# Graph network on one core: search for node ends inside the first attention stage, longer lags and a batch ring in the edge stages, bank halves in a normalisation

## What is computed

```python
# layer 0, attention, summed by src over 4 heads
scores = clip(einsum('ehd,ehd->eh', q[src], k[dst]), -10, 10)
w = exp(scores) / segment_sum(exp(scores), src)[src]
x = layernorm(2 * x + segment_sum(w * v[dst], src))
# layer 1, sum: relu(x[src] + attr @ We + be) summed by dst, two matmuls, batch norm, relu
# layer 2, max: twice leaky_relu(segment_max(x[src] @ Wm + attr @ We, dst) + x @ Wr + b)
# layer 3, attention by dst: e = exp(leaky(a_src[src] + a_dst[dst]) - segment max)
out = tanh(segment_sum(h[src] * e, dst) / segment_sum(e, dst) + bias)
```

## Time and profile before

| | |
|---|---|
| time, median of 3 runs | 11399.82 us (11399.76 to 11401.9) |
| the profiled execution: run, span | 11406.15 us, 11404.3 us |
| busy share PE / PEld / DVE / ACT / POOL | 39% / 26% / 58% / 12% / 71% |
| granted TensorE clock, mean | 0.56 of full speed |
| DMA, mean over the span | 111 GB/s |
| e0, 578 to 2698 us | DMA engines 78% busy, 203 GB/s |

### The profile page before, as it was taken

One profiled execution on the slowest core, in us unless ns is written; L12 is line 12 of the kernel. 1 busy time (PEld: TensorE's weight loads), 2 busy tenths in 40 slices (PEclk: granted clock), 3 DMA queues, 4 the chain that ended last, 5 costly groups with the idle time before them and its releaser, 6 DMA issues. The chain is left out here.

```text
span 11404.3 us, 81326 instructions
## 1 busy us (share of the span) xinstructions
PE 4465.4 (39%) x15877; PEld 3003.7 (26%) x15877; DVE 6589.5 (58%) x11020; ACT 1415.8 (12%) x3304; POOL 8115.1 (71%) x8559
## 2 busy tenths in 40 slices
PE   3167666663222222243232323332323234444443
PEld 3066656662111111121111111111111123333332
DVE  9966666666555555555555555555555555555555
ACT  3011111111000000010000000000000023333333
POOL 2177777776777777757777776777777777777776
PEclk8555555555555555565555555555555555555665
DMA  3177788774333333323333333333333323333332
GB/s 96 57 200 206 205 203 205 205 204 124 98 99 98 99 99 98 91 71 98 100 98 99 98 100 80 98 99 99 98 99 98 95 60 81 82 82 81 81 83 68
DMA packets 1061469, 1264.91 MB, mean 111 GB/s; under 512 B 489075, under 2 KB 841315, under 8 KB 1060611
## 3 DMA queue, kind: packets, MB, share of 16 engines
q0 software_dynamic: 303968, 521.40, 20.5%
q1 hardware_dynamic: 638571, 636.33, 17.4%
q10 hardware_dynamic: 118432, 101.99, 3.6%
HBM read 830.35 MB, written 428.44 MB: 110 GB/s over the span
## 5 line engine op out<-in xcount | busy, mean ns | idle before, releaser
L825 POOL DMA_INDIRECT e_got<-kv_tab,dst_cols x1664 | 1584.1, 952 | 518.1 <-issue 507.3
L1106 POOL DMA_INDIRECT e2a_got<-x_tab,src_cols x1616 | 1524.8, 944 | 566.6 <-issue 566.6
L1763 POOL DMA_INDIRECT e_got<-h_tab,src_tcols x1616 | 1532.4, 948 | 502.5 <-issue 502.5
L1106 POOL DMA_INDIRECT e2b_got<-x_tab,src_cols x1616 | 1524.8, 944 | 512.0 <-issue 512.0
L1106 POOL DMA_INDIRECT e_got<-x_tab,src_cols x1616 | 1524.7, 944 | 507.3 <-issue 507.3
L835 PE MATMUL e_Q<-e_window,e_pick 128*128 128x96 f32 x3328 | 797.3, 418 | 696.9 <-issue 442.5
L1122 PE MATMUL e_EA<-we_We,e_attr 128*128 128x384 f32 x808 | 577.4, 870 | 1072.3 <-DVE e_emsg L1141 1072.3
L1122 PE MATMUL e2a_EA<-we_W_edge,e2a_attr 128*128 128x384 f32 x808 | 579.9, 873 | 1056.5 <-DVE e2a_emsg L1141 1056.5
L1122 PE MATMUL e2b_EA<-we_W_edge,e2b_attr 128*128 128x384 f32 x808 | 581.0, 874 | 1051.7 <-DVE e2b_emsg L1141 1051.7
L835 PEld LDWEIGHTS e_Q<-e_window,e_pick 128*128 128x128 f32 x3328 | 713.9, 317 | 803.2 <-issue 600.2
L1141 DVE TENSOR_TENSOR e2b_emsg<-e2b_EA,e2b_got 128x768 f32<-128x768 f32 x202 | 192.9, 955 | 728.4 <-issue 711.5
(11 more groups left out here) (368 smaller groups left out, 10371.3 us busy)
## 6 DMA issues: line engine op xcount, KB each, us to landing
scan_out<-e_out SPq DMA_DIRECT2D x416, 200.0 KB
e_window<-q_tab SPq DMA_DIRECT2D x1664, 48.0 KB
scan_out<-e_out SPq DMA_DIRECT2D x404, 196.0 KB
scan_out<-e_out SPq DMA_DIRECT2D x202, 384.0 KB
scan_out<-e2a_out SPq DMA_DIRECT2D x202, 384.0 KB
scan_out<-e2b_out SPq DMA_DIRECT2D x202, 384.0 KB
e_rel<-rel_row ACTq DMA_DIRECT2D x416, 128.0 KB
e_keep<-keep_row ACTq DMA_DIRECT2D x416, 100.0 KB
```

Of the source, the lines that this page charges most:

```text
L825: e.indirect_dma_start(got[u][:, k, :], None, kv_tab, bass.IndirectOffsetOnAxis(dst_c[:, c * K + k:c * K + k + 1], axis=0)).then_inc(s_g[u ...
L1106: e.indirect_dma_start(got[s % RS][:, k, :], None, x_tab, bass.IndirectOffsetOnAxis(src_cols[:, q:q + 1], axis=0)).then_inc(edge_got[s % R ...
L1763: e.indirect_dma_start(got[c % RG][:, k, :], None, h_tab, bass.IndirectOffsetOnAxis(src_tcols[:, q:q + 1], axis=0)).then_inc(s_g[c % RG], 16)
```

## The change

- find0 disappears as a stage; its work runs inside e0. The first src of each chunk is taken from first_row. ScalarE instead of VectorE counts, with Sign and an accumulator: one row count per chunk at chunks 8 to 56, one count in a gathered row at every second chunk from 84. GpSimd issues a search gather after the chunk's four at every second chunk from 80. VectorE makes the masks at chunk 6 and the ends at chunk 186. The masks' loads are issued by SP behind the windows of chunk 3, their stores behind those of chunk 39.
- In e0 the gather ring has six chunks, pick, rel and pay four buffers, the scan runs three chunks behind, queries three ahead, one-hot four ahead, SP's stores 13 behind the windows; a mask row holds two chunks.
- n3b hands over by halves (tiles 0 to 3, 4 to 6): matmuls, statistics, table and X.
- e3: gathers go straight into a ring of three batches (12 chunks), `hold` and its copies are gone; 1612 instead of 1616 gathers. Batch it is worked out in four pieces between the four chunks of batch it-1. The scan runs two chunks behind, the copies out further, and weights go to SBUF through ACT.
- In prep one GpSimd operation on 49 columns is dropped (node_q keeps its half).

```diff
-        with Phase("find0", group="node") as ph:
...
-        with Phase("e0", group="edge") as ph:
+        with Phase("e0", group="edge") as ph, Phase("find0", group="node") as pf:
+            QL, SL, RG0 = 3, 3, RG
...
+            ROWS_AT, GOT_AT, KEEP_AT = 8, 80, 6
+            COUNT_AT = GOT_AT + 4
+            END_AT = COUNT_AT + 2 * NT + 4
...
                 @block.sync
+                    BEHIND = 13
                     for c in range(NCH0):
...
-                        if c >= U:
-                            store(c - U)
+                        if c >= BEHIND:
+                            store(c - BEHIND)
+                        if c == U - 1:
+                            e.dma_start(dst_i[:, :], t["dst_pad"].rearrange("(p c) -> p c", p=P)).then_inc(s_dst, 16)
+                            e.dma_start(prev_i[:, :], t["dst_prev"].rearrange("(p c) -> p c", p=P)).then_inc(s_dst, 16)
...
                 @block.gpsimd
                     for c in range(NCH0):
-                        after(e, v_pay, c - U + 1)
+                        after(e, v_pay, c - RG0 + 1)
...
+                        if GOT_AT <= c < GOT_AT + 2 * NT and (c - GOT_AT) % 2 == 0:
+                            q = (c - GOT_AT) // 2
+                            e.wait_ge(a_row, q // G + 1)
+                            after(e, a_cnt, q - G + 1)
+                            e.indirect_dma_start(found[:, q % G, :], None, src_lin.rearrange("(r c) -> r c", c=CH),
+                                                 bass.IndirectOffsetOnAxis(row_i[:, q:q + 1], axis=0)).then_inc(row_got[q % G], 16)
...
                 @block.tensor
                     for c in range(NCH0):
...
-                        if c > 0:
-                            turn_back(c - 1)
-                        if c + 2 < NCH0:
-                            queries(c + 2)
+                        if c + QL < NCH0:
+                            queries(c + QL)
+                        if c >= SL:
+                            turn_back(c - SL)
...
                 @block.vector
-                        if c + 2 < NCH0:
-                            picks(c + 2)
-                        if c > 0:
-                            scan(c - 1)
+                        if c + 4 < NCH0:
+                            picks(c + 4)
+                        if c >= SL:
+                            scan(c - SL)
+                        if c == KEEP_AT:
+                            masks()
+                        if c == END_AT:
+                            ends()
...
                 @block.scalar
+                        if ROWS_AT <= c < ROWS_AT + NT:
+                            rows_of(c - ROWS_AT)
+                        if COUNT_AT <= c < COUNT_AT + 2 * NT and (c - COUNT_AT) % 2 == 0:
+                            count((c - COUNT_AT) // 2)
...
             with Phase("n3b", group="prep") as p2:
...
+                HALVES = ((0, 4), (4, G))
...
-                            after(e, a_x, it - 1)
-                            after(e, v_tab, it - 1)
-                            for g in range(G):
-                                q = it * G + g
-                                ins = e.matmul(raw(it, g), xT_all[:, q * P:(q + 1) * P], Wyi[:, :], start=True, stop=True)
-                            ins.then_inc(t_out, 1)
+                            for h, (lo, hi) in enumerate(HALVES):
+                                after(e, a_x, 2 * it + h - 3)
+                                for g in range(lo, hi):
+                                    q = it * G + g
+                                    ins = e.matmul(raw(it, g), xT_all[:, q * P:(q + 1) * P], Wyi[:, :], start=True, stop=True)
+                                ins.then_inc(t_out, 1)
...
         with Phase("e3", group="edge") as ph:
...
                 @block.gpsimd
+                    for q in range(TILES):
+                        it, c = q // BT, q // K
+                        if q % K == 0:
+                            after(e, v_add, c - RB * U + 1)
+                        e.indirect_dma_start(got[:, q % (RB * BT), :], None, h_tab, bass.IndirectOffsetOnAxis(src_tcols[:, q:q + 1], axis=0)).then_inc(s_g[it % RB], 16)
...
                 @block.vector
...
+                    batch = (logits, carries, maxima, factors)
+                    for it in range(NI + 1):
                         for u in range(U):
+                            c = (it - 1) * U + u
+                            if it > 0:
+                                add(c)
+                                if c > 1:
+                                    scan(c - 2)
+                            if it < NI:
+                                batch[u](it)
```

More of the change, by code:

```diff
@@ L1792, in batch, with spread @@
-                    def batch(it):
-                        H.wait(e, f"hold{U - 1}", it)
-                        TB.give(e.transpose(ST, hold[:, :, D + 1], ident[:, :]), "scores")
+                    def spread(c):
+                        it, u = c // U, c % U
+                        if u == 0:
+                            VB.wait(e, "low", it)
+                        after(e, v_scan, c - 2)
+                        for k in range(K):
+                            e.matmul(Z[c % 3][0:HW, k * P:(k + 1) * P], sel[:, u * K + k, :], parts[it % 2][:, :], start=True, stop=True)
@@ L1902, in body, with factors @@
[L1902 to L1910 removed]
+                    def factors(it):
+                        p = parts[it % 2]
+                        e.wait_ge(a_exp, it + 1)
+                        op(e.tensor_copy(p[0:BT, :], wd[:, 1, :]), it, "high")
+                        op(e.tensor_tensor(z[:, :], wd[:, 1, :], p[0:BT, :], ALU.subtract), it, "rest")
+                        op(e.tensor_copy(mid[:, :], z[:, :]), it, "mid")
+                        VB.give(e.tensor_copy(p[32:32 + BT, :], mid[:, :]), "mid32")
+                        VB.give(e.tensor_tensor(p[64:64 + BT, :], z[:, :], mid[:, :], ALU.subtract), "low")
@@ L1928, in body @@
-                    def body(it):
-                        for u in range(U):
-                            if not isinstance(it, int) or it > 0:
-                                step(it, u)
-                            c = it * U + u
-                            e.wait_ge(s_g[c % RG], got_before[c % RG] + 16 * K * (c // RG + 1))
-                            V[u].wait(e, "add", it, 1)
-                            H.give(e.activation(hold[:, u * K:(u + 1) * K, :], got[c % RG][:, :, :], ACT.Copy), f"hold{u}")
-                        VB.wait(e, "d", it)
-                        H.give(e.activation(wd[:, :, :], wd[:, :, :], ACT.Exp), "exp")
@@ L1938, in _, with to_out, message @@
-                    loop(e, NI, body, apart=4)
-                    for u in range(U):
-                        step(NI, u)
-                    to_out(NI + 1, 0)
+                    def to_out(c):
+                        e.wait_ge(t_back, c + 1)
+                        if c >= U:
+                            e.wait_ge(s_st[c % U], 16 * (c // U))
+                        e.activation(out[c % U][:, :, :], B[c % 2][:, 0:K * HW].rearrange("p (k d) -> p k d", k=K), ACT.Copy).then_inc(a_out, 1)
+                    def message(c):
+                        e.wait_ge(t_fwd, c + 1)
+                        after(e, v_scan, c - 2)
+                        e.activation(msg[c % 3][:, :], M[c % 2][0:HW, :], ACT.Copy).then_inc(a_msg, 1)
@@ new lines, in _ @@
+                    for it in range(NI + 1):
+                        for u in range(U):
+                            c = (it - 1) * U + u
+                            if c > 0:
+                                message(c - 1)
+                            if c > 3:
+                                to_out(c - 4)
+                            if u == 2 and it < NI:
+                                VB.wait(e, "d", it)
+                                e.activation(wd[:, :, :], wd[:, :, :], ACT.Exp).then_inc(a_exp, 1)
+                        if it < NI:
+                            TB.wait(e, "weights", it)
+                            e.activation(wts[it % 2][:, :], WT, ACT.Copy).then_inc(a_wt, 1)
@@ L1944, in build @@
+                    message(NCH - 1)
+                    for c in range(NCH - 4, NCH):
+                        to_out(c)
         with Phase("n7", group="node") as ph:
```

584 lines of the change are left out of this document (279 added, 305 removed).

## The result

The changed kernel takes 11480.5 us (median of 4 runs, 11479.1 to 11483.2) beside 11400.1 us for the kernel before on the same chip: ratio 1.007, 95% interval 1.0058 to 1.0082. A second set on another chip gave 11467.5 against 11398.8, ratio 1.0062 (1.0046 to 1.0079). The prediction of 11356 was wrong in its sign. The profiled execution spans 11479.1 us, against 11404.3.

What follows compares the result with a forecast made beforehand. GpSimd's issue of gathers was taken to bound the edge stages. Search and e0 -37.6, n3b -6 and e3 -0.3 summed to -43.9 us, giving 11356 us; range 11338 to 11380.

Steps and rivals of the forecast that it cites:

- the ring gives nothing inside: In e3, a ring of batches saves nothing between gathers; only four padding gathers left out, -5.0 us.
- Rival 3: In e0, VectorE's comparison L865 locks onto GpSimd's gather beat, 0.25 us per hit: 11445 us, slower; chance 0.03.
- Search in e0: Removing find0 puts e0's first gather at about 488.6, 89.7 us earlier; 49 search gathers add 61.6 us.
- e0's pitch: Without 5 us of stalls, e0's gathers come every 1.2567 us, the last at 2641.7, 31.6 us earlier.
- the interference: In e0, gather time above 1.25 us per step while VectorE works, within the 1.2567; masks add 1.6 us once.
- rival 2: In e0, SyncE's window loads take GpSimd's place as the bound: +27 us, 11383, no change; chance 0.09.
- e0's drain: From e0's last gather to the node stage's first: 18.4 us instead of 24.45, 6.0 gained; bounds 0 and 8.
- Search and e0 together: Removing find0, adding search gathers to e0, removing its stalls and shortening its end: -37.6 us in sum.
- n3b: Normalisation by halves: about 5.5 us per tile group instead of 6.42; -6 us in all, bounds -2 and -9.
- No table loads: In e0, Sign among the Exps costs no table load; chance 0.01 that loads appear after all.
- the rule that was weighed: Function-set switches on ScalarE cost about 2.7 us each; Sign beside Exp in e0 would add about 120 us.
- e3's drain: After e3's last gather, interleaving adds 6.7 us and an earlier copy saves 1.6; some 34 us long.

Runs made afterwards that it cites:

- the run with both edits: Changed kernel with e3's weights read from PSUM and VectorE's burst 0.6 us later: 11375.0 us, ratio 0.998 to the kernel before.
- e3_old: Changed kernel with the last edge stage put back as before: 11381.6 us, ratio 0.9981; 13193.2 us, 0.9967 on the first slow chip.
- before_sbuf: Kernel before, with e3's weights copied from PSUM to SBUF and read there: 11448.7 us, ratio 1.0045, where the kernel before takes 11400.

## Why the prediction was wrong, point by point

- **The step that failed** is "GpSimd did not wait before, so the ring gives nothing inside" e3. The first half was true. The conclusion looked only at waits between gathers, and priced the edit that comes with the ring, weights copied out of PSUM so that two batches can be in flight, at nothing. The prediction knew the row that spoke against it: the earlier trace rows has a gather of 1.20 us under the comparison L865. It took that for a matter of one operation of e0 and didn't go through the operands of each VectorE operation that the change rewrites. The page that it cited, the Trainium skill ("GPSIMD Engine Reference", section "Specifications"), names two SBUF inputs as a second ground of contention beside the two-port modes, in the same line; only the first was weighed.
- **Rival 3 had the mechanism, in the wrong stage.** VectorE did lock onto GpSimd's beat and cost about 0.25 us and more per hit; its 11445 was 35 us short. It happened in e3, where the burst follows the landing of the batch's last gather at a fixed distance, and so met a gather's start in every batch. A chance of 0.03 was far too small for a cause of which the trace held samples.
- **Search in e0:** first gather 488.9 (488.6 predicted). Right.
- **e0's pitch:** GpSimd's stalls went, as predicted: no gap between gathers above the usual 0.30 us. But the last gather came at 2651.9 instead of 2641.7. The term that was mis-sized is the interference, taken as unchanged: 145 long gathers with 21.4 us of excess instead of 104 with 10.8. One of them takes 3.67 us where the masks are made, 2.7 us above the usual where 1.6 was allowed. Gathers also start under the comparison more often, 143 of 1713 instead of 104 of 1664. That the deeper queue puts them there is my reading; no run tried it.
- **SyncE (rival 2):** not the bound. Its wait for ScalarE's copies did not go, as predicted, but rose from 15.6 us to 43.0. ScalarE's copies in turn waited 265 us for SyncE's stores, which are issued 13 chunks behind the windows while a copy needs the store of four chunks back landed. The prediction foresaw neither, and GpSimd waited for neither.
- **e0's drain:** 19.5 us, 18.4 predicted; the product came 5.1 us behind the last gather, not 4.0.
- **Search and e0 together:** -26.3 us instead of -37.6. The sum kept bounds for the drain and none for the pitch, where 10 of the 11 us went.
- **n3b:** standard deviations 5.49 us apart (about 5.5 predicted), 11.0 for two groups instead of 12.84:

```profile
4893.91 0.33 ACT L1376 ACTIVATE n3b_std<-n3b_mv,eps_col 128x7 f32<-128x7 f32 x1
...
4899.40 0.33 ACT L1376 ACTIVATE n3b_std<-n3b_mv,eps_col 128x7 f32<-128x7 f32 x1
...
4904.89 0.33 ACT L1376 ACTIVATE n3b_std<-n3b_mv,eps_col 128x7 f32<-128x7 f32 x1
```

  From its first operation to e2a's first gather the stage took 47.7 us instead of 53.9, so it gained 6.1 us, and 6.0 in the second trace; 6 was predicted. Right. That the table at the top shows only 4.2 us behind e0 is due to 2 us lost ahead of n3b in the first trace.
- **No table loads** appear in e0 (the second of the trace is at 2668.2 us, behind it): Sign beside Exp cost nothing, as argued from the trace against the rule that was weighed.
- **e3's drain:** 28.8 us (11355.14 to 11383.95) instead of 34. The first weighted message of the last batch came 13.0 us after the last gather, 12.4 before; the interleaving's price was right in kind, but the burst starts 3 us earlier without ScalarE's copy, and the four chunks then follow 1.72 us apart. A miss of 5 us, with no weight in the result.

Added up: -26.3 up to the end of e0, -5.0 from there to e3, +106.5 inside e3, -0.4 in its drain: +74.8 us, the difference of the two profiled spans (11479.1 - 11404.3). The medians are 80 apart.

## What to carry to other kernels

Where GpSimd issues gathers back to back and is the bound, a VectorE instruction with two inputs in SBUF is a possible hold of up to its own length, and so can be one with a single SBUF tile, such as e0's comparison; operations that follow each other without a gap can count as one. Not every kind does it: of 77 gathers that started in the first 0.2 us of e0's reduce (L889, input in SBUF) none was held. Before moving a PSUM operand to SBUF for the sake of a deeper pipeline, list the operands of what runs beside the gathers; here a copy to another PSUM bank kept two batches in flight and took 85 us less than the copy to SBUF. And look at the mean duration of the bounding engine's instructions, not only at its waits: a hold shows up as a longer instruction and as idle time nowhere.

## What was not expected of the hardware

- A chain of four VectorE operations (0.41, 0.25, 0.15 and 0.54 us) held one gather 0.85 us, although the reduce among them has a single input. In some batches GpSimd got through between the copy and the weighting (1.31 us instead of 1.8), and with the copy and the weighting on PSUM it got through after the scan (0.97 to 1.13 us). Why it sometimes slips in and mostly not stays open.
- Small operations count: the running-maximum scan over 16 partitions and 128 columns held a gather by 0.16 to 0.18 us when it had run for 0.11 to 0.12 us (78 of 78 in the changed kernel). When it had run for 0.10 us or less no gather was held (79 of 79 before); the scan then took up to 0.55 us instead of 0.47.
- The step is sharp, and its place depends on the operation: for the difference L1925 in the run with both edits it lies between a lead of 0.03 us (gather 0.94, operation 0.35 instead of 0.27) and one of 0.04 (gather 1.05, operation 0.27).
- A gather can also be held without a two-input operation under its start: in the kernel before, 38 of 48 that started 0.21 to 0.31 us into e0's reduce L889 were long, up to 1.07 us. Whether the reduce or the operations behind it did that stays open.
- Loss and gain hang on tenths of a microsecond: the changed kernel lost 118.9 us by this in one trace and 105.1 in the next, with the burst 0.05 us elsewhere.
- On three chips the kernel before took 13.2 to 13.4 ms instead of 11.4, and in the kernels traced there GpSimd waited for buffers at the same cost of a gather (956 ns in e3 of e3_old). There an edit worth 50 us elsewhere (before_sbuf) could not be measured: 0.9993 and 1.0002.
